# First attention layer of a graph network: the sum of the softmax weights by GpSimd's additions and two matmuls a chunk, in place of twenty matmuls a chunk

## The reference

```python
h = maximum(layernorm(x), 0)
# attention layer (4 heads of 512; then 1 head of 768, mean over heads)
h = (h @ W).reshape(N, H, C)
e = leaky_relu(al_s[src] + al_d[dst], 0.2)      # al_s, al_d: h against att_src, att_dst
ex = exp(e - segment_max(e, dst)[dst])
denom = segment_sum(ex, dst)
out = segment_sum(h[src] * (ex / (denom[dst] + 1e-16))[:, :, None], dst) + bias
# x = x + attention2(elu(attention1(h)))
# x = x + gcn(relu(gcn(maximum(layernorm(x), 0)))), gcn: symmetric norm, h @ W, segment_sum, bias
```

## Time and profile before

| | us |
|---|---|
| three runs, median | 1415.37 (1415.19 to 1418.91) |
| span of the profiled execution, first to last instruction | 1413.8 |
| TensorE busy | 1258.0 |
| VectorE busy | 976.1 |
| ScalarE busy | 538.2 |
| GpSimd busy | 51.8 |

### The profile page before, as it was taken

One profiled execution on the slowest core, in us unless ns is written; L12 is line 12 of the kernel. 1 busy time (PEld: TensorE's weight loads), 2 busy tenths in 40 slices (PEclk: granted clock), 3 DMA queues, 4 the chain that ended last, 5 costly groups with the idle time before them and its releaser, 6 DMA issues. The chain is left out here.

```text
span 1413.8 us, 23848 instructions
## 1 busy us (share of the span) xinstructions
PE 1258.0 (89%) x8102; PEld 1172.2 (83%) x8103; DVE 976.1 (69%) x2279; ACT 538.2 (38%) x1205; POOL 51.8 (4%) x44
## 2 busy tenths in 40 slices
PE   2698989998939999999999999983999699998998
PEld 2576757667938999999999999983999699988998
DVE  7898988976968668776776678777867644354231
ACT  1322222212337548555566556514543321133110
POOL 6000000000020000000000000000000400000000
PEclk9999999996559999999999999996999899999999
DMA  5031203012021001101010200001200210141001
GB/s 177 16 105 39 105 38 105 33 42 75 0 68 46 1 19 58 46 1 61 16 45 1 75 1 1 1 0 40 82 1 1 90 45 29 40 136 61 24 30 37
DMA packets 31570, 63.34 MB, mean 45 GB/s; under 512 B 5010, under 2 KB 10170, under 8 KB 31456
## 3 DMA queue, kind: packets, MB, share of 16 engines
q1 hardware_dynamic: 30176, 55.26, 11.7%
q0 software_dynamic: 1088, 6.29, 1.3%
q10 hardware_dynamic: 192, 0.32, 0.1%
HBM read 43.70 MB, written 18.17 MB: 44 GB/s over the span
## 5 line engine op out<-in xcount | busy, mean ns | idle before, releaser
L1086 PE MATMUL p_a<-ring_hi,hs 128*128 128x256 f32 (+1 forms) x1600 | 320.8, 284 | 11.7 <-DVE hs L944 8.4
L1086 PEld LDWEIGHTS p_a<-ring_hi,hs 128*128 128x128 f32 x1600 | 263.3, 192 | 14.5 <-issue 8.7
L1086 PE MATMUL p_a<-ring_lo,hs 128*128 128x256 f32 (+1 forms) x800 | 225.4, 282 | 0.0
L1547 PE MATMUL p_y<-cr_hi,g_hi 128*128 128x256 f32 (+1 forms) x600 | 150.2, 291 | 18.7 <-ACT cr_hi L1406 15.1
L715 ACT ACTIVATE e<-p_shift,al_h 128x256 f32<-128x256 f32 (+1 forms) x400 | 153.2, 488 | 7.3 <-PE p_shift L700 4.9
L1086 PEld LDWEIGHTS p_a<-ring_lo,hs 128*128 128x128 f32 x800 | 154.8, 194 | 0.0
L1547 PE MATMUL p_y<-cr_hi,g_lo 128*128 128x256 f32 (+1 forms) x600 | 149.1, 289 | 0.0
L473 DVE TENSOR_SCALAR hot<-iota,key x488 | 144.6, 296 | 1.4 <-issue 1.4
L1547 PEld LDWEIGHTS p_y<-cr_hi,g_hi 128*128 128x128 f32 x600 | 120.3, 201 | 20.4 <-ACT cr_hi L1406 19.9
L723 ACT ACTIVATE ring_hi<-pf 128x512 fp32r<-128x512 f32 (+1 forms) x125 | 80.0, 640 | 143.8 <-DVE pf L734 129.8
L471 DVE TENSOR_SCALAR hot<-iota,low 125x128 uint16 x488 | 121.2, 248 | 10.8 <-issue 7.5
(11 more groups left out here) (221 smaller groups left out, 2483.9 us busy)
## 6 DMA issues: line engine op xcount, KB each, us to landing
h_scratch<-stage SPq DMA_DIRECT2D x40, 256.0 KB, 2.1
hs<-h_scratch SPq DMA_DIRECT2D x40, 256.0 KB, 2.8
w_st<-in_L_gnn_W SPq DMA_DIRECT2D x4, 1536.0 KB, 9.6
w_st<-in_L_gnn_W POOLq DMA_DIRECT2D x4, 1536.0 KB, 7.0
gw_st<-in_L_gnn_W SPq DMA_DIRECT2D x12, 384.0 KB, 3.1
xr<-in_x SPq DMA_DIRECT2D x9, 384.0 KB, 7.1
rows<-in_x SPq DMA_DIRECT2D x9, 384.0 KB, 3.7
g_scratch<-orow SPq DMA_DIRECT2D x18, 192.0 KB
```

Of the source, the lines that this page charges most:

```text
L1086: nc.tensor.matmul(p_a[:, f, 0:n], hs[:, s, a, cols], r, start=s == 0 and j == 0, stop=s == T - 1 and j == 2)
L1547: last = nc.tensor.matmul(p_y[:, f, 0:n], hs[a][:, s, f * P:(f + 1) * P], c_hi[:, i % RS, s % G, 0:n], start=s + a == 0, stop=s == T - 1 a ...
```

## The change

In the first layer the twenty ones-matmuls of a chunk go. GpSimd adds the five weight groups of a chunk elementwise, with four additions (`add_up`), into one of three buffers `dens` of 2 x 256 columns. At the end of the chunk TensorE multiplies ones with the two halves, in full float32, into `p_den`. Normalizing waits for that. Weighing waits, before it overwrites a buffer of `pf`, until the addition that reads it is done (`pf_free`): group 2 and group 3 of a chunk for addition 1, group 4 for addition 2, and, outside a head's first chunk, group 0 for addition 3 of the chunk before and group 1 for addition 4. The W2 loads move from GpSimd's queue to SyncE's: the first ahead of the head loop, each later one ahead of that head's row loads. The scratch for software-made DMA descriptors is set to 8192.

```diff
+    dens = sb("dens", [P, 3, G, CW], fp32)
+    added = sem("added")
+    dens_step, dens_ready, den_done = sem("dens_step"), sem("dens_ready"), sem("den_done")
...
+            def load_weights(h):
+                sp.wait_ge(wlo_done, h * KH + 1)
+                sp.dma_start(w_st[:, :, :], W2v[:, bass.ds(h, 1), :, :].rearrange("p a k n -> p (a k) n")).then_inc(w_in, 16)
+
+            load_weights(0)
             with sp.Fori(1, HEADS) as h:
+                load_weights(h)
                 for t in range(T):
...
             nc.gpsimd.memset(rows[:, :, :], 0.0).then_inc(zeroed, 1)
+            def add_up(h, c, g):
+
+                n = CHUNKS[c][1]
+                q = h * NC + c
+                acc = dens[:, c % 3, :, 0:n]
+                pool_.wait_ge(wt.pf_ready, q * NG + g + 3)
+                if g == 1:
+                    pool_.wait_ge(den_done, q + 1)
+                    first = wt.pf[:, (c * NG) % 2, :, 0:n]
+                else:
+                    pool_.wait_ge(dens_step, q * (NG - 2) + g - 1)
+                    first = acc
+                ins = nc.gpsimd.tensor_tensor(acc, first, wt.pf[:, (c * NG + g) % 2, :, 0:n], ALU.add)
+                ins.then_inc(dens_ready if g == NG - 1 else dens_step, 1)
+                pool_.wait_ge(dens_ready if g == NG - 1 else dens_step, (q + 1) if g == NG - 1 else q * (NG - 2) + g)
+                pool_.sem_inc(added, 1)
+
             with pool_.Fori(0, HEADS) as h:
-                pool_.wait_ge(wlo_done, h * KH + 1)
-                pool_.dma_start(w_st[:, :, :], W2v[:, bass.ds(h, 1), :, :].rearrange("p a k n -> p (a k) n")).then_inc(w_in, 16)
+                for c in range(NC):
+                    for g in range(1, NG):
+                        add_up(h, c, g)
...
-                dve.wait_ge(wt.used, (q + 2) * NG)
+                dve.wait_ge(den_done, q + 3)
                 nc.vector.reciprocal(rden[:, 0:n], p_den[:, 0:n]).then_inc(rden_done, 1)
...
+            def pf_free(h, c, g):
+
+                q = h * NC + c
+                dve.wait_ge(added, q * (NG - 1) + 2 + ((0 if c == 0 else -1), 0, 1, 1, 2)[g])
+
...
                     for g in range(NG - 1):
+                        pf_free(h, c, g)
                         wt.weigh(nc, dve, counts, q, c, g)
...
+                    pf_free(h, c, NG - 1)
                     wt.weigh(nc, dve, counts, q, c, NG - 1)
...
-                            nc.tensor.matmul(p_a[:, f, 0:n], hs[:, s, a, cols], r, start=s == 0 and j == 0,
-                                             stop=s == T - 1 and j == 2)
-                    for j, r in enumerate((hi, lo)):
-                        last = nc.tensor.matmul(p_den[:, 0:n], ones_r[:, :], r, start=s == 0 and j == 0,
-                                                stop=s == T - 1 and j == 1)
+                            last = nc.tensor.matmul(p_a[:, f, 0:n], hs[:, s, a, cols], r, start=s == 0 and j == 0,
+                                                    stop=s == T - 1 and j == 2)
...
+                pe.wait_ge(dens_ready, q + 1)
+                for i in range(G):
+                    last = nc.tensor.matmul(p_den[:, 0:n], ones_r[:, :].bitcast(fp32), dens[:, c % 3, i, 0:n],
+                                            start=i == 0, stop=i == G - 1)
+                last.then_inc(den_done, 1)
...
-    nc = bacc.Bacc("TRN2", target_bir_lowering=False, num_devices=1)
+    nc = bacc.Bacc("TRN2", target_bir_lowering=False, num_devices=1, dynamic_dma_scratch_size=8192)
```

More of the change, by code:

```diff
@@ L842, in _ @@
                 sp.dma_start(abc[:, a, :], vec.to_broadcast([P, D])).then_inc(a_in, 16)
+            W2v = W2.rearrange("(h k p) n -> p h k n", p=P, h=HEADS)
+            def load_weights(h):
+                sp.wait_ge(wlo_done, h * KH + 1)
+                sp.dma_start(w_st[:, :, :], W2v[:, bass.ds(h, 1), :, :].rearrange("p a k n -> p (a k) n")).then_inc(w_in, 16)
+            load_weights(0)
             with sp.Fori(1, HEADS) as h:
+                load_weights(h)
                 for t in range(T):
@@ L852, in _ @@
             nc.gpsimd.memset(rows[:, :, :], 0.0).then_inc(zeroed, 1)
-            W2v = W2.rearrange("(h k p) n -> p h k n", p=P, h=HEADS)
+            def add_up(h, c, g):
[13 more added lines that the diff above has]
+                pool_.sem_inc(added, 1)
             with pool_.Fori(0, HEADS) as h:
-                pool_.wait_ge(wlo_done, h * KH + 1)
-                pool_.dma_start(w_st[:, :, :], W2v[:, bass.ds(h, 1), :, :].rearrange("p a k n -> p (a k) n")).then_inc(w_in, 16)
+                for c in range(NC):
+                    for g in range(1, NG):
+                        add_up(h, c, g)
         @block.scalar
@@ L935, in _ @@
             dve.sem_inc(wlo_done, 1)
+            dve.sem_inc(added, 2)
             dve.sem_inc(z_done, 1)
@@ L1070, in _ @@
             pe.sem_inc(wt.e_ready, 1)
+            pe.sem_inc(den_done, 2)
             pe.sem_inc(wt.used, NG)
```

## The result

The changed kernel takes **1441.91 us** (median; 1441.15 to 1442.88) against 1417.14 (1415.19 to 1418.96) for the kernel before, run beside it: a ratio of 1.0166 [1.0149, 1.0183]. The medians lie 24.8 us apart; their quotient, 1.0175, is inside that interval. (The ratios with their intervals are estimated over the runs and need not be the quotient of two medians.) The forecast was 1435 with a range of 1393 to 1445. The profiled execution took 1442.24 with a span of 1440.5, 26.7 more than the span of 1413.8 before.

The account below looks back on a forecast made before the run. TensorE was taken to bound most intervals, with little VectorE slack. Interval changes summed to +24.3 us, less 4 for product waits, clock 0: +20 on 1415.4 gave 1435 us, range 1393 to 1445.

Parts of the forecast that it names:

- TensorE's saving: Each chunk, ones-matmuls of 2.4 us give way to two float32 matmuls of 1.1: 1.3 us less, 26 us in all.
- rival A: Additions neither hold VectorE up nor keep group 2 waiting long, so TensorE's gain stays: -20, 1395 us; chance 25%.
- Addition 1: GpSimd's addition of weights 0 and 1; group 2's weighing waits for it, VectorE standing idle: +1.4 us a chunk.
- Addition 2: Ready during the next low part, it enters the 0.04 us gap within the next weighing: +1.3 us, or 0.
- Addition 4: Starts in the 0.52 us gap ahead of oT's low part on VectorE: +0.8 us, in chunk 0 +1.3.
- The intervals of head 1: Interval k ends in chunk k+1's reciprocal; each lasts as the later of TensorE (25.0 us) and VectorE: +3.2 a head.
- the clock at 0: TensorE's half clock after stalls over 3 us, 1.6 us each, mostly hidden behind VectorE: 0, up to +10 for the range.
- Rival C: The clock falls too: stalls of seven or eight intervals each pass 1.6 us on, +10 more, 1446 us; chance 10%.
- The start: The way to head 0's first reciprocal holds additions 1, 2, 4, 1, 2, less 0.7 of slack: +6.0 us.
- The -4 for waits on products: VectorE's 66.6 us of waits for TensorE's products partly vanish where VectorE comes late, in ten intervals: -4 us.
- B: Only the wait counts, VectorE always winning the port: 1.4 us a chunk, 0.8 before oT's low part; 1414 us, chance 17%.
- D: SyncE's queue, with the W2 loads, holds row loads back, so heads start late: +5 us a head; chance 1%.

## Why the forecast held, step by step

- **TensorE's saving** was right in kind, small in size: the intervals that TensorE bounds fell from 26.32 to 24.71 us, 1.6 and not 1.3. The term that was off is the two float32 matmuls at 1.1 us: 2.4 less 1.6 leaves 0.8 (their first record starts at 628.56, the products behind them at 629.24). With nothing else changed that was 24.5 us in all instead of rival A's 20.
- **W2 on SyncE** at 0: right, 0.9995 [0.9982, 1.0008].
- **Length of an addition**, 1.3 us: right, 1.30 alone. Beside two-input operations the record says 1.66, some 0.5 of it waiting. The prediction put an addition of 1.1 us at about 3 us less in all; by its own 1422 for 0.9 us it would be some 6.
- **Addition 1**, +1.4: 1.35 measured. **Addition 2**, +1.3: 1.1, but in the wrong place. GpSimd does not need the 0.04 us gap between L732 and L734, where I put it; it gets in at the edge behind the low part, though VectorE's operations there are back to back, and L732 pays. The sign I named, an L734 of 1.5 us, never came. My reading of the earlier trace rows, that GpSimd gets in only where VectorE leaves a gap, is thereby wrong. **Addition 3**, 0: right but for the very first chunk. **Addition 4**, +0.8 in the gap ahead of oT's low part: it is 0.98 on average, at the ELU step, one operation earlier. The sum of 3.5 us a chunk stands, at 3.4, outside chunk 0. There additions 1 and 2 meet the split of hidden rows, which the prediction did not look at, at 1.1 us each (two splits take 2.38 us there and took 1.28).
- **The intervals of head 1** were forecast at 26.9, 28.8, 25.6, 25.0 and 28.9 and measured at 28.37, 28.26, 28.10, 24.71 and 29.11. Two are off, 0 and 2, and in both the granted clock was 0.88. With the idle time filled they are 26.07 and 25.27. The step that failed is thus the clock at 0 ("most is hidden as VectorE is the later one"): the slowed matmuls are the products for which VectorE itself waits. Rival C's mechanism was real in head 1, at 2.3 to 2.8 us a place. That the total of 1442 lay within the range is partly luck: this term was put at 0, the -4 below did not come, and TensorE's saving was larger than forecast.
- **The start**, +6.0 forecast from five additions at 1.3 and 1.4 less the slack: from the first weighing to the first reciprocal it is 24.11 us before and 29.58 after, +5.5. It took six additions at some 1.1 each, as in the first chunk addition 3 meets the split too (four splits in one line, before and after):

```profile
423.57 2.49 DVE L944 TENSOR_TENSOR hs<-hs 128x512 fp32r<-128x512 f32 x4
425.40 3.59 DVE L973 TENSOR_TENSOR hs<-hs 128x512 fp32r<-128x512 f32 x4
```

  Two errors cancel here, one addition too few and each of them too dear. Without additions the same stretch is 23.35 us and beside free ones 29.30.
- **Heads**: first reciprocal +5.1 (forecast +6.0), head 0 -0.6 (+1.4), heads 1 and 2 together +6.9 (+6.4), head 3 +13.9 (+10.5), behind the last reciprocal +1.4: +26.7 on the span. Heads 1 and 2 agree by two errors: head 1 took +6.6 and head 2 +0.3. In the kernel before, interval 0 of head 2 is 28.94 us, 3 more than head 1's, and I read only head 1; there TensorE stands for 2.6 us where the loop body starts over, and in the changed kernel that stall (2.46 us) is hidden behind a late VectorE. Head 3 came out 3.4 above its forecast: intervals 0, 2, 3 and 4 took +1.7, +3.7, +4.2 and +2.5 against +1.0, +2.9, +3.4 and +0.8. All four hold a stall of 2.6 to 4.0 us with a low clock behind it; filling it in 0 and 2 gave back 1.1 and 1.3, and for 3 and 4 the cause stays open.
- **The -4 for waits on products** did not come: those waits grew from 66.6 us to 77.2, in part for the slowed products: with the idle time filled they are 72.3.
- **Rivals.** A is out (the additions cost 46.7 us), B is out (four buffers win 2.7 us and not 20), D is out. The collision alone gives 40.2 of the 46.7 us.
- **Open**: why the first weighing starts anywhere between 412.8 and 420.9 us in the twelve profiles, one of each kernel; it shifts all times behind it and is no part of the change. That reading from two sides at once is what collides follows from the three kinds of operation; which port it is, no run shows.

## What to carry to other kernels

Before work is handed to GpSimd, ask what VectorE does at that moment: next to operations with two inputs in SBUF, GpSimd's reading is added to VectorE's time even where GpSimd is idle for 88% of the span and nothing waits for it. The same 80 additions cost 31 us less when three of four were held until VectorE read PSUM, which took more buffers and a wait on the right semaphore. And work taken from the bounding engine is worth at most the other engine's slack, so read that slack interval by interval, in every head, and not in one.

## What the runs showed of the hardware beyond that

- GpSimd gets its turn at the edge between two back-to-back VectorE operations: the addition issued at 626.71 is still running when the low part ends at 627.23, and the L732 behind it lasts 1.78 us instead of 0.69.
- The hold is shorter than GpSimd's record and goes with what it reads: 0 for a memset of 0.53 us, 0.38 for one input of 512 elements (record 0.89), 0.98 for two (record 1.6).
- VectorE's operations with one input in SBUF and one in PSUM keep their length beside an addition: `z` 416 ns, `rows` 550, against 415 and 551.
- Two full-float32 matmuls of 256 columns, shown as four records, took TensorE 0.7 to 0.8 us where 1.1 was expected from the earlier trace rows.
- In the changed kernel's first layer, from head 1 on, TensorE's granted clock was 0.50 to 0.54 in the 3 us behind idle times of 3.06 to 3.98 us, 0.66 behind one of 2.60 (at 822.64) and 1.00 behind one of 2.46 (at 681.88). The length of the idle time alone does not decide it: with four weight buffers the clock was 1.00 behind 2.88 us (at 611.08) and 0.50 behind 2.85 (at 743.88).
